# Block addresses of a graph kernel's edge stages, packed four to a word and unpacked in registers

## The reference, cut to what matters

```python
edge_index = jnp.stack([src, dst])
h = relu(layernorm(x))
x = x + attention(h, Wq, bq, Wk, bk, Wv, bv, src, dst)      # 8 heads of 32
h = relu(layernorm(x))
x = x + hyperbolic_messages(h, weight, edge_index, ...)     # sums over edges by src

# attention
scores = einsum('ehd,ehd->eh', q[src], k[dst]) / sqrt(32)
e = exp(scores - segment_max(scores, dst)[dst])
p = e / segment_sum(e, dst)[dst]
out = segment_sum(v[src] * p[:, :, None], dst)

# messages
x_local = logmap(x[row], x[col])
att = sigmoid(silu(cat[x_tangent[row], x_tangent[col], distances] @ att_w1 + att_b1) @ att_w2 + att_b2)
agg = segment_sum(x_local * att, row) / 100
```

## Time and profile before

| what | value |
|---|---|
| time of three runs | 4219.08, 4187.47, 4195.17 us; median 4195.17 |
| span of the profiled execution | 4137.2 us |
| runs less that span | 50 to 82 us, 58 at the median |
| attention stage | about 700 to 2160 us of the span |
| messages stage | about 2325 to 3940 us |
| TensorE / VectorE busy over the span | 73% / 82% |

### The profile page before, as it was taken

One profiled execution on the slowest core, in us unless ns is written; L12 is line 12 of the kernel. 1 busy time (PEld: TensorE's weight loads), 2 busy tenths in 40 slices (PEclk: granted clock), 3 DMA queues, 4 the chain that ended last, 5 costly groups with the idle time before them and its releaser, 6 DMA issues. The chain is left out here.

```text
span 4137.2 us, 55464 instructions
## 1 busy us (share of the span) xinstructions
PE 3002.7 (73%) x12662; PEld 2413.6 (58%) x12662; DVE 3401.4 (82%) x9121; ACT 2194.8 (53%) x5961; POOL 1969.1 (48%) x2404
## 2 busy tenths in 40 slices
PE   3545444577777777677756688988988888888866
PEld 2434333455555555555545567777777777777754
DVE  8999996687888888788878378888888888888877
ACT  3235542444444444444438466666665666666557
POOL 1000003556666666666620366666666666666400
PEclk9867777788998889888988899999999999999988
DMA  2111004666667666666636655655655666556361
GB/s 65 39 55 38 13 26 148 191 202 208 202 208 216 207 209 208 211 205 209 206 98 174 172 161 168 173 163 168 171 168 167 167 172 170 166 167 170 89 145 50
DMA packets 295230, 635.60 MB, mean 154 GB/s; under 512 B 78197, under 2 KB 147123, under 8 KB 294657
## 3 DMA queue, kind: packets, MB, share of 16 engines
q0 software_dynamic: 141312, 463.96, 38.3%
q1 hardware_dynamic: 153602, 168.11, 14.5%
HBM read 587.26 MB, written 44.65 MB: 153 GB/s over the span
## 5 line engine op out<-in xcount | busy, mean ns | idle before, releaser
L2469 POOL DMA_INDIRECT area<-d_xr,col x880 | 890.2, 1012 | 686.8 <-DVE area L2706 236.8
L2562 PE MATMUL ms_near_a<-low,ms_hotT 128*128 x1760 | 550.4, 395 | 204.3 <-issue 99.2
L2066 PE MATMUL at_out<-at_pv,at_hot 128*128 128x264 f32 x1760 | 558.6, 447 | 75.7 <-issue 32.0
L2020 POOL DMA_INDIRECT low<-d_qv,col x440 | 449.6, 1022 | 265.6 <-DVE at_pv L2196 129.1
L2563 PE MATMUL ms_near_c<-tab_c,ms_hotT 128*128 x1760 | 536.1, 387 | 0.0
L2046 PE MATMUL at_kx<-area,tab_c 128*128 x1760 | 508.8, 417 | 21.8 <-issue 20.7
L2562 PEld LDWEIGHTS ms_near_a<-low,ms_hotT 128*128 128x128 f32 x1760 | 327.6, 192 | 301.6 <-issue 258.9
L2066 PEld LDWEIGHTS at_out<-at_pv,at_hot 128*128 128x128 f32 x1760 | 358.9, 217 | 161.9 <-issue 63.1
L2046 PEld LDWEIGHTS at_kx<-area,tab_c 128*128 128x128 f32 x1760 | 372.9, 213 | 96.0 <-issue 25.3
L2238 DVE SCALAR_TENSOR_TENSOR area<-area,tab_c,at_out 128x264 f32 x440 | 211.7, 481 | 216.4 <-remote 114.9
L2604 ACT COPY area<-area 128x2 f32<-128x2 f32 x440 | 82.0, 186 | 566.0 <-DVE area L2675 379.0
(11 more groups left out here) (375 smaller groups left out, 6560.6 us busy)
## 6 DMA issues: line engine op xcount, KB each, us to landing
tab_c<-by_dst_marks SPq DMA_DIRECT2D x110, 512.0 KB
ms_near_no<-by_src_near SPq DMA_DIRECT2D x110, 224.0 KB
area<-d_xr,col POOLq DMA_INDIRECT x880
d_qv<-low SPq DMA_DIRECT2D x10, 1120.0 KB, 5.0
low<-d_qv,col POOLq DMA_INDIRECT x448
d_xr<-mid_hm SPq DMA_DIRECT2D x5, 1128.8 KB, 6.8
first_x<-in_x_dram SPq DMA_DIRECT2D x5, 1120.0 KB
tab_c<-in_x_dram SPq DMA_DIRECT2D x5, 1120.0 KB, 7.0
```

The lines of the kernel that those rows point to most:

```text
L2020: pool.indirect_dma_start(out=ring[t.n % SLOTS][:, k, :], out_offset=None, in_=m.d_qv, in_offset=bass.IndirectOffsetOnAxis(ap=col[:, t.h, ...
L2066: last = TE.matmul(out[:, p % 2, 0:AW], hot[:, t.h % 2, j, :], pv[:, t.h % 2, j].rearrange("p h d -> p (h d)"), start=(k == 0), stop=(k == ...
L2469: pool.indirect_dma_start(out=far_rows(t, p)[:, k, :], out_offset=None, in_=m.d_xr, in_offset=bass.IndirectOffsetOnAxis(ap=col[:, t.h, SPA ...
L2562: TE.matmul(near_a[:, (SPAN * p + k) % 4, 0:TW], rows, m.tab_a[:, bass.ds(at, TW)], start=True, stop=True)
```

## The change

The list `off` is no longer read. At the start of each stage VectorE makes a table of 110 whole numbers, one for each group, from the block numbers that it already has: bits 0 to 5 hold the block of the group's first step, and three fields of two bits hold how many blocks further on steps 1, 2 and 3 are. TensorE and VectorE load one such word for a group and work out the block of a step from it in registers: a mask for step 0, and a shift and a mask for steps 1 to 3, then an addition and the multiplication by the stride, which join the address's FUSED_REGOPS.

```diff
-class Starts:
...
-        self.eng.load(self.regs[0:n], self.off[0:1, bass.ds(at, n)])
...
-        return [self.eng.snap(r, min_val=0, max_val=self.top) for r in self.regs[first:first + n]]
...
+class Plan:
...
+    def fetch(self, t):
+
+        reg = self.regs[t.n % len(self.regs)]
+        self.eng.load([reg], self.words[0:1, t.n:t.n + 1])
+        self.word[t.n % len(self.regs)] = self.eng.snap(reg, min_val=0, max_val=(1 << Plan.BITS) - 1)
+
+    def start(self, t, p):
+
+        word = self.word[t.n % len(self.regs)]
+        block = word & 63
+        if p:
+            block = block + ((word >> (4 + 2 * p)) & 3)
+        return block.with_bounds(min_val=0, max_val=NB - 1) * self.stride
+
+
+def make_words(dve, V, ln, words, blk, work):
...
+    steps = blk.rearrange("o (g j) -> o g j", j=SG)
+    first, total, more = steps[:, :, 0], work[0], work[1]
+    for j in range(1, SG):
+        ln.mark(V.tensor_tensor(more[j - 1], steps[:, :, j], first, ALU.subtract))
+    ln.wait()
+    ln.mark(V.scalar_tensor_tensor(total, more[0], 64.0, first, ALU.mult, ALU.add))
+    ln.wait()
+    ln.mark(V.scalar_tensor_tensor(total, more[1], 256.0, total, ALU.mult, ALU.add))
+    ln.wait()
+    ln.mark(V.scalar_tensor_tensor(words, more[2], 1024.0, total, ALU.mult, ALU.add))
+    ln.wait()
...
@@ -1994,7 +2020,6 @@
-                sp.dma_start(off[:, :], edges.off[0:1, 0:SUPER]).then_inc(c_in, 16)
...
-                pe.wait_ge(c_in, 32)
+                pe.wait_ge(planned, 1)
...
-                dve.wait_ge(c_in, 32)
+                dve.wait_ge(c_in, 16)
+                ln = Links(dve, word)
...
+                make_words(dve, V, ln, words[:, :], blk[0:1, 1:1 + SUPER], spare_row)
+                dve.sem_inc(planned, 1)
...
@@ -2025,18 +2050,18 @@
-                    if p % 2 == 0:
-                        starts.fetch(t.n * SG + p, 2)
-                    at = starts.values(p % 2, 1)[0]
+                    if p == 0:
+                        plan.fetch(t)
+                    at = plan.start(t, p)
...
@@ -2287,15 +2316,13 @@
                     if old.exists():
-                        starts.fetch(old.n * SG, SG)
-                        at = starts.values(0, SG)
+                        plan.fetch(old)
...
@@ -2706,12 +2733,14 @@
+                    if p == 0:
+                        plan.fetch(t)
                     n = t.n * SG + p
                     dve.wait_ge(out_in, n + 1)
-                    row = m.acc_l1[:, bass.ds(at, TW)]
+                    row = m.acc_l1[:, bass.ds(plan.start(t, p), TW)]
...
-                        if done.exists():
-                            add(done, q, starts.values(q, 1)[0])
-                        if p == 2 and old.exists():
-                            starts.fetch(old.n * SG, SG)
+                        add(done, q)
```

More of the change, by code:

```diff
@@ L1807, in _, with __init__ @@
                         project(n, p2[:, n % 2, 0:DIM], sT, 1, proj2)
-class Starts:
[L1813 to L1817, removed]
-        self.eng.load(self.regs[0:n], self.off[0:1, bass.ds(at, n)])
-    def values(self, first, n):
-        return [self.eng.snap(r, min_val=0, max_val=self.top) for r in self.regs[first:first + n]]
-    def load(self, at, n):
-        self.fetch(at, n)
-        return self.values(0, n)
+class Plan:
+    BITS = 12
+    def __init__(self, eng, tag, words, stride, keep):
+        self.eng, self.words, self.stride = eng, words, stride
+        self.regs = [eng.alloc_register(name=f"{tag}_word{n}") for n in range(keep)]
+        self.word = {}
+    def fetch(self, t):
[20 more added lines that the diff above has]
+    ln.wait()
 SUPER = ET // SPAN + NB - 1
@@ L2027, in _ @@
                 TE = nc.tensor
-                pe.wait_ge(c_in, 32)
+                pe.wait_ge(planned, 1)
                 pe.wait_ge(made, 7)
-                starts = Starts(pe, "at_pe", off, (NB - 1) * AW, 2)
+                plan = Plan(pe, "at_pe", words, AW, 2)
                 def near(t, p):
@@ L2234, in add @@
                     dve.wait_ge(out_in, t.n * SG + p + 1)
-                    row = m.acc_l0[:, bass.ds(at[p], AW)]
+                    row = m.acc_l0[:, bass.ds(plan.start(t, p), AW)]
                     if p or t.plus(-1).exists():
@@ L2536, in _ @@
                 TE = nc.tensor
-                pe.wait_ge(c_in, 80)
-                starts = Starts(pe, "ms_pe", off, (NB - 1) * TW, 2)
+                pe.wait_ge(c_in, 64)
+                pe.wait_ge(planned, 1)
+                plan = Plan(pe, "ms_pe", words, TW, 2)
                 def near(t, p):
@@ L2791, in _ @@
                 hot_columns(Turn(0, 0))
-                dve.wait_ge(c_in, 80)
+                dve.wait_ge(c_in, 64)
+                ln = Links(dve, word)
+                rows = dd[1].rearrange("p k c -> p (k c)")[0:1]
+                rows = [rows[:, n * AGROUPS:(n + 1) * AGROUPS] for n in range(SG)]
+                make_words(dve, V, ln, words, blk[0:1, 1:1 + SUPER], (rows[0], rows[1:]))
+                dve.sem_inc(planned, 1)
                 V.tensor_tensor(keep[:, :], blk[:, 1:1 + SUPER], blk[:, 0:SUPER], ALU.is_equal).then_inc(made, 1)
@@ L2796, in _ @@
                 dve.wait_ge(made, 3)
-                starts = Starts(dve, "ms_dve", off, (NB - 1) * TW, SG)
+                plan = Plan(dve, "ms_dve", words, TW, 1)
                 hot_columns(Turn(0, 1))
```

35 lines of the change are left out of this document (17 added, 18 removed).

## The result

| kernel | median, us | runs |
|---|---|---|
| before | 4195.09 (4178.26 to 4219.08) | 20 |
| changed | 4210.42 (4200.57 to 4229.64) | 20 |

The ratio is **1.0031, 95% interval 1.0015 to 1.0046**: some 13 us slower. The forecast was 4221 us and within 1%.

What follows compares the result with a forecast made beforehand. TensorE and VectorE hand work to each other in both edge stages, so what executes between a wait's end and the work counts. Terms -6 + 14 + 12 + 5 + 1 = +26 us took 4195 to about 4221 us, range 4165 to 4277.

Steps and rivals of the forecast that it cites:

- Register instructions behind `near`'s wait in the messages, +12 us: TensorE in messages: 128 waits x 0.18 = 23.0 us more idle time, about half on the path, +12 us.
- VectorE's add in the attention, +14 us: Attention add, L2238: 107 waits x 0.18 = 19.3 us of register instructions, three quarters paid, +14 us.
- TensorE in the attention, 0: Attention, `near`: waits are over early, half a group before the bank is wanted, so register instructions cost nothing.
- The exposed load, -6 us: Messages, VectorE's load ahead of L2706: 12.7 us of "issue" goes, perhaps half only passed on, -6 us (0 to -12.7).
- VectorE's add in the messages, +5 us: Messages, 93 waits ahead of the add: 8 to 17 us of delay, less than half reaching the end, +5 us.
- The starts, +1 us: Start of each stage: six small VectorE operations, 1.2 us, against the saved copy of `off`; +1 us for both (-2 to +3).
- The prices: Both engines: a one-number load about 0.31 us; each register instruction 0.09 us (0.03 to 0.12), two making 0.18 us.
- The time around the span, 58 us: Outside the profiled span of 4137.2 us: 58 us at the median of the runs, untouched by the change.
- all of it is hidden: Rival, both stages: late releases and idle time absorb the 0.18 us delays; 4195 us, within -12 and +10; chance 0.23.
- The one in which the load doesn't shrink: Rival, load ahead of messages' first add: one number still takes 0.6 us, 33 us in all, 4254 us; chance 0.04.
- Serial and dear: Rival, `near` and `add`: all 328 waits on the path at 0.24 us, 79 us, 4277 us; chance of over +1% 0.22.
- The fourth: Rival, both stages: loads were on the path, "issue" waits shrink; -52 us, 4143 us; chance of gain over 1% 0.11.

Runs made afterwards that it cites:

- before again: The kernel before, unchanged, compared with itself under the slower conditions (before at 4138 us): ratio 1.0002 (0.9982 to 1.0021).
- short dose: The kernel before plus one fused register instruction behind near's last wait, TensorE, messages only; against before at 4138 us: ratio 1.0023 (1.0007 to 1.0040).
- first two comparisons: Two of the three follow-up comparisons, each of four kernels against before, which takes 3703.56 us in the first and 3704.20 in the second.
- with the addresses ahead: Whole change, but each address worked out into its own register ahead of the step's waits; against before: 3693.40 against 3703.56 us, ratio 0.9972.
- one such version: Packed number on TensorE only, addresses worked out ahead of near's waits, VectorE as before; against before at 4138 us: ratio 1.0082 (1.0056 to 1.0108).
- long dose: Before plus five fused register instructions, against before at 3704 us: behind near's last wait in messages on TensorE 1.0185; between the attention add's waits on VectorE 1.0732.

## Why the prediction was right, and where not

The forecast of a small loss, inside 1%, came true: +13 to +16 us where +26 was summed. Its two engines' shares did not, and that the sum came near owes something to luck: nearly all of the +14 us for VectorE's add did not come, and the -6 us for the load, which did not come either, made up for a part of that. By terms, with the stage lengths under the faster conditions, while the prediction worked from a profile under the slower ones:

- *Register instructions behind `near`'s wait in the messages, +12 us:* right in mechanism, place and size. 13.8 us with messages changed alone, 14.2 us with PE changed alone. Its working was less so: 128 waits were counted from four rows and halved for the path, because VectorE waits less often. Under the faster conditions there are 110 waits, one in each group; half of them end with ScalarE and cost nothing more, and the 55 that end with VectorE pay 0.23 us each, 12.7 us in all. The check by the first profile (204 us to about 227) gave only 98.8 + 59.5 + 34.7 + 17.1 = 210.1; the engine's idle time shows first ahead of the weight load, and that row, which I had not used, grew from 258.9 to 269.6 us.
- *VectorE's add in the attention, +14 us:* the failed step. It took 107 waits at 0.18 us as paid to three quarters. Alone it costs 0.6 us, and both engines' parts together 3.7 and 6.8 us in two kernels. The 0.18 us is right. That it lies on the path is not, under the faster conditions: there most adds follow an operation that covers it, and the add waits for TensorE only 43 times for 25.1 us and never for "remote", in the profile with the old attention. The "remote" part of the 107 waits belongs to the slower conditions, under which VectorE's part alone, with the instructions behind the waits, was not run. There the term is untested. The check I had named, 210 us growing to 230, read 286.0, and tells little: the kernel before read 210.3, then 216.1 (again), and the one with the short dose, whose attention is the same, 244.4.
- *TensorE in the attention, 0:* 1.1 us alone. Right.
- *The exposed load, -6 us:* the load went as said, from 12.7 us of "issue" to none. The gain was nothing: the wait for `near` took 12.2 of the 12.7 us. I had halved it for the row that showed the next wait 0.22 us long; read as it stands, all of it was passed on.
- *VectorE's add in the messages, +5 us:* 2.5 us for VectorE's whole part, in which the load's gain was nothing. Two profiles of unchanged messages lie 2.1 us apart, so all that is shown is that the term is small.
- *The starts, +1 us:* the stretch ahead of the attention is 705.9 to 707.9 us in all kernels of the first two comparisons, without order. Unmeasurable, as forecast.
- *The prices:* 0.30 us for a load of one number (0.31 forecast). For a register instruction 0.09 us was taken from one start to the next; 36 and 45 ns of work with gaps between them come to 0.1 us on PE (2706.1, 2706.2 and 2706.3 above). Right.
- *The time around the span, 58 us:* wrong, it is 2. The 58 us were the difference between the profiled execution and the runs. It cancelled here, as only differences were added.

Of the rivals, "all of it is hidden" reached up to 4205 us; the median is 4210 and the interval of the ratio leaves out 1, so it is out, though not by much. The one in which the load doesn't shrink is out by 0.30 us. The Trainium skill (DMA: Bandwidth & Descriptors, "Latency and other measured facts") puts a floor of about 600 ns under it, and the trace does not agree. The Trainium skill (Runtime: NRT & Kernel Launch, "Instruction fetch mechanics") also gives about 200 ns for each register, of the loads that the runtime puts in; for the kernel's own loads here 301, 516 to 520 and 946 ns for one, two and four numbers make 0.215 us for each beyond the first, so with that the trace agrees. "Serial and dear" would have needed the 107 and 93 waits of VectorE on the path. The fourth, that the loads were on the path, may have some truth: with the addresses ahead, 6 us are won in the attention, perhaps by the shorter loads. The rule I forecast by, that in such a loop only what stands between a wait's end and the work counts, is what the version ahead of the waits shows under the faster conditions. It needs an addition: it counts only behind the wait that holds up the loop.

## What to carry to other kernels

Behind a wait that holds up the loop, register arithmetic for an address cost its full length (0.22 us of 0.22, and 1.2 of 1.2); ahead of the waits it cost nothing under the faster conditions. Where a compiler works an expression out at its use, pin it into a register at the place where you want it paid, and measure, as one such version lost 38 us for a reason that is open. Before costing a delay, look at the operation in front of it on the same engine: it hides at most its own length. And ask of each wait which engine ends it: two waits at the same line can be worth one delay or nothing.

## What the runs showed of the hardware

**One program, two speeds.** The same kernel takes 3704 us in two comparisons and 4138 to 4195 us in two others. It is not the chip: one and the same gave 3703.56 us and, half an hour later, 4137.62. The difference is in the two edge stages, here the rows of windows for two kernels (change in the attention only; before again), each window being that stage:

```profile
707.00:1914.00 1207.00, 969.70 (x3960) 752.51 (x3960) 1142.82 (x2310) 666.65 (x1429) 898.59 (x864) 0.93 0.79 240
2096.00:3504.00 1408.00, 1357.34 (x6160) 1158.09 (x6160) 1333.68 (x4838) 1009.00 (x3245) 1037.65 (x1477) 1.00 0.66 186
```

```profile
705.00:2146.00 1441.00, 1027.88 (x3960) 782.01 (x3960) 1148.70 (x2311) 667.54 (x1429) 881.28 (x864) 0.88 0.67 201
2326.00:3922.00 1596.00, 1410.66 (x6160) 1183.50 (x6160) 1340.60 (x4838) 1010.85 (x3245) 1039.44 (x1477) 0.97 0.59 164
```

VectorE, ScalarE and GpSimd are busy for the same time to 2% in stages that are 234 and 188 us longer. For these three all of it is waiting; TensorE is also busy 58 and 53 us longer. Ahead of `near` in the messages 98.1 us become 249.8, and ahead of the attention's add stand waits for "remote", which the faster conditions do not show:

```profile
DVE area L2238 <- remote: 104.6, 33, 6.5
```

TensorE's mean granted clock is lower there (0.88 against 0.93 in the attention, 0.97 against 1.00 in the messages), in stretches in which it stood idle more. What arrives late is not settled. For whoever compares pages: two profiles can differ by more than the change under study, so check a profiled execution against the timed runs first, and take stage lengths from kernels of one comparison.

**A fused register instruction has no fixed price.** On PE it took from 37 ns for the shortest to 232 ns in the long dose, on VectorE from 46 to 283, so a count of instructions says little about their cost.
